# First edge layer of a graph network on one core: where VectorE builds the matrix of equal owners within a round

## The reference, cut to what matters

```python
Wh = h @ W + b
Wr, Wc = Wh[row], Wh[col]
sim = sum(Wr * Wc) / maximum(norm(Wr) * norm(Wc), EPS)
base = adj_v * sc * (row != col)
prop_pos = segment_sum((base * relu(sim))[:, None] * Wc, row)
prop_neg = segment_sum((base * -relu(-sim))[:, None] * Wc, row)
x = x + scale * (coeff[0] * prop_pos + coeff[1] * prop_neg + coeff[2] * Wh)
```

## Time and profile before

| what | value |
|---|---|
| median of three executions | 2410.95 us |
| the profiled execution, its own time | 2418.68 us |
| its span | 2416.6 us |
| busy, share of the span | PE 65%, DVE 64%, ACT 36%, POOL 70% |
| first edge layer, in the trace | about 206 to 1503 us of the span |
| POOL busy from 500 to 1500 us | 809.97 us of 1000 |
| DVE busy from 500 to 1500 us | 514.08 us of 1000 |
| granted TensorE clock from 500 to 1500 us | 0.50 |

### The profile page before, as it was taken

The page is one execution under the profiler, slowest core; times in us unless marked ns, Lnnn a source line. Parts: engine busy times, 40 slices in busy tenths (PEclk is TensorE's granted clock), DMA queues, the critical chain, the costliest instruction groups (busy, mean ns, idle before and its releaser), DMA issues. The chain is left out here.

```text
span 2416.6 us, 57279 instructions
## 1 busy us (share of the span) xinstructions
PE 1562.8 (65%) x16004; PEld 1340.6 (55%) x16004; DVE 1553.3 (64%) x5636; ACT 864.0 (36%) x3093; POOL 1695.9 (70%) x1413
## 2 busy tenths in 40 slices
PE   4886755455555555555555550005999999997998
PEld 2555645455554545545455550004999999994554
DVE  5995655555555454554545552794999999995554
ACT  3773322222222222222222221462333333334665
POOL 2775888888888888888888886746777777761322
PEclk9996555555555555555555555556999999999999
DMA  3775544444444444444444432565555454534664
GB/s 100 251 247 172 114 82 80 77 83 75 84 79 78 84 74 85 80 77 83 75 86 73 84 47 18 170 221 146 128 124 126 124 126 124 126 81 119 188 188 145
DMA packets 342563, 273.11 MB, mean 113 GB/s; under 512 B 144834, under 2 KB 273514, under 8 KB 342484
## 3 DMA queue, kind: packets, MB, share of 16 engines
q1 hardware_dynamic: 259028, 233.22, 33.2%
q0 software_dynamic: 81536, 38.61, 15.0%
q10 hardware_dynamic: 1920, 0.37, 0.1%
HBM read 206.69 MB, written 65.34 MB: 113 GB/s over the span
## 5 line engine op out<-in xcount | busy, mean ns | idle before, releaser
L1117 POOL DMA_INDIRECT x<-e_sums,e_to x392 | 623.4, 1590 | 126.4 <-issue 118.6
L1352 PE MATMUL bank<-e_parts,e_same 128*128 128x64 bf16 x2940 | 172.8, 240 | 586.7 <-DVE e_parts L1211 586.7
L1304 PE MATMUL bank<-e_window,e_onehot 128*128 128x64 f32 x2352 | 525.0, 422 | 16.8 <-DMA e_window<-wh 16.8
L1304 PEld LDWEIGHTS bank<-e_window,e_onehot 128*128 128x128 f32 x2352 | 511.7, 332 | 16.9 <-DVE e_onehot L1143 16.9
L1102 POOL DMA_INDIRECT e_ends<-wh,e_ids x392 | 425.2, 1085 | 132.8 <-issue 102.1
L1352 PEld LDWEIGHTS bank<-e_parts,e_same 128*128 128x128 bf16 x2940 | 159.4, 129 | 602.8 <-issue 602.8
L829 POOL DMA_INDIRECT e_near_source<-h,e_near_ids x392 | 394.8, 1007 | 129.8 <-issue 117.4
L1250 ACT ACTIVATE e_sq<-e_ends 128x64 f32<-128x64 f32 x784 | 188.6, 241 | 686.0 <-DMA e_ends<-wh,e_ids 685.9
L1175 DVE SCALAR_TENSOR_TENSOR e_prod<-e_ends 128x64 f32<-128x64 f32 x392 | 65.7, 223 | 370.8 <-DMA e_ends<-wh,e_ids 370.8
L939 PE MATMUL bank<-e_near_to_edge,e_near_window 128*64 128x128 f32 x2352 | 153.4, 281 | 171.2 <-DMA e_near_window<-h 171.2
L939 PEld LDWEIGHTS bank<-e_near_to_edge,e_near_window 128*64 128x64 f32 x2352 | 130.0, 139 | 177.6 <-DVE e_near_to_edge L850 171.6
(11 more groups left out here) (150 smaller groups left out, 2860.9 us busy)
## 6 DMA issues: line engine op xcount, KB each, us to landing
e_window<-wh SPq DMA_DIRECT2D x392, 96.0 KB
e_near_window<-h SPq DMA_DIRECT2D x392, 96.0 KB
e_owners<-ends SPq DMA_DIRECT2D x98, 256.0 KB, 2.9
n_x<-x SPq DMA_DIRECT2D x98, 256.0 KB, 3.0
n_x<-in_x_dram SPq DMA_DIRECT2D x49, 256.0 KB, 2.8
wh<-n_wh SPq DMA_DIRECT2D x49, 256.0 KB, 2.0
x<-n_x SPq DMA_DIRECT2D x49, 256.0 KB, 2.3
e_rel<-rel SPq DMA_DIRECT2D x98, 128.0 KB, 3.2
```

The costliest lines, as they stand in the source:

```text
L1117: pool.indirect_dma_start(out=added_tab, out_offset=bass.IndirectOffsetOnAxis(ap=t.to[s][:, j:j + 1], axis=0), in_=t.sums[s][:, j, :], in_ ...
L1304: last = nc.tensor.matmul(bank[s % 2][:, j * D:(j + 1) * D], onehot, window, start=w == 0, stop=w == WK - 1)
L1352: last = nc.tensor.matmul(bank[6 + s % 2][:, i * D:(i + 1) * D], t.same[s][:, same_block(j, i), :], t.parts[s][:, part, j, :], start=j == ...
```

## The change

In DVE's list for the first edge layer the part `compare` now comes before `match`, with every lag as it was. So in step i DVE first makes the dot products of group i-2 and then the matrix of equal owners of group i-1. It used to be the other way round.

```diff
-        parts = [(-3, leave), (0, ahead), (-3, low), (-1, match), (-2, compare), (-2, address), (-2, weigh)]
+        parts = [(-3, leave), (0, ahead), (-3, low), (-2, compare), (-1, match), (-2, address), (-2, weigh)]
```

## The result

The changed kernel takes 2393.63 us in the median of five runs (2391.51 to 2400.18), the kernel before 2411.21 us in the same comparison. The ratio is 0.9921, with a 95% interval from 0.9903 to 0.9938. By this ratio it is 19 us faster, between 15 and 23. (The medians alone differ by 17.6 us.) The forecast was 2392 us.

The account below looks back on a forecast made before the run. POOL's own instructions bound the first edge layer, lengthened 0.63 us a round by DVE running beside them. With 0.43 us instead, 0.20 us less over 94 rounds is 19 us: 2410.95 to 2392 us, range 2372 to 2427 us.

Parts of the forecast that it names:

- DVE's chain: DVE's work from `weigh` on comes 0.95 us later; T is the first dot product's start; DVE does not become the bound.
- The landing: Loads issued earlier no longer lie beside the last gather, so L falls to 2.4 to 3.0 us in most rounds.
- L: Time from the start of a round's last gather to the dot products; sets where DVE's work falls on POOL's.
- The third scatter: At L = 2.5 us POOL's third scatter starts at T+2.55 in the last `same`, losing 0.1 us.
- The rival in which scatters pay more than gathers save: Landing stays; third scatter starts in the 384-column `same`, second gather in the one-hot; 5 to 15 us slower; chance 0.28.
- The rival in which the whole matrix blocks a scatter: A scatter loses to all four `match` rows, 1.1 us a round; 80 us slower, 2491 us; chance 0.03.
- The sum: POOL's surplus from running beside DVE falls from 0.63 to 0.43 us a round, 19 us over 94 rounds; chance 0.43.
- theory 3: From the experiments: taking the matrix of equal owners off the gathers is the gain, whatever L is.
- theory 4: Formed after e8: the one-hot's place against the first gather is what changed; long gathers come from one-hot with `low` behind.
- `match` costs the gathers 0.25 us a round: Surplus before: 0.12 us on the third gather, 0.10 us on 27 long gathers, 0.03 us on the gather behind.
- the balance of 0.24 us on scatters against 0.25 us on gathers: With places spread evenly, `match` costs scatters now what it cost gathers; the no-change rival, 2411 us, chance 0.18.
- list for each L: Loss a round by L: 0.3 us at 2.5, 0.4 or 0.5 at 2.9, 0.9 at 3.5, about 0.2 above 4.2.

Follow-up runs that it names:

- e2: Changed kernel with SP's owners load and those behind it held until `low` of the slot's last group is done; ratio 1.0007, 13.08 us a round.
- e1: Kernel before, with SP's owners load and those behind it released early, once the slot's last addresses are written; ratio 1.0052, 13.21 us a round.
- e8: Kernel before with the matrix of equal owners cut to 8 columns per instruction, so sums are not the layer's; ratio 1.0017, 13.06 us a round.
- e9: Changed kernel with the matrix cut to 8 columns per instruction, so sums are not the layer's; 2411.27 us, ratio 0.9984, 13.10 us a round.
- e10: e1 with the left-over computed twice more, 0.7 us more DVE work ahead of the one-hot; 2385.92 us, ratio 0.9881, 12.78 us a round.
- e5: The changed kernel itself again, on another chip; ratio 0.9895, 12.89 us a round.
- e7: Changed kernel with the two address instructions ahead of the matrix instead of behind it; ratio 0.9962, 12.88 us a round.
- e6: Changed kernel reordered: dot products, matrix, row numbers and one-hot, weighing, then addresses; ratio 0.9860, 12.66 us a round.

## Why the prediction was right, and where it wasn't

**The bound and the mechanism: right.** POOL's own instructions and the constant gaps between them are the length of the layer, before and after (226.7 and 226.8 us of gaps), and the change acted through the instructions' lengths alone.

**DVE's chain: right.** `weigh` starts at T+3.03 (T+3.25 forecast), the one-hot at T+6.23 (T+6.15), and the norms are no wait any more. `weigh`'s second instruction, which takes 0.17 us alone, takes 0.45 us in the rounds shown, so the 0.2 us by which it started early were lost again behind it. The cover held: ACT, PE and SP lost nothing that POOL saw.

**The landing: right.** L fell from 3.55 to 2.49 us, and 92 of 93 rounds are under 3.3 us. `owners` is issued at T+2.9, as forecast.

**The third scatter: right, and cheap.** It starts at T+2.57 (T+2.55) in the last `same` and loses 0.04 us in the mean; I had 0.1 us. The rival in which scatters pay more than gathers save needed L over 3.2 us, and e2 shows a piece of it: at L up to 3.3 us and more the period is 13.08 us. The rival in which the whole matrix blocks a scatter is refuted by the rows at 577.23: 0.49 us lost of 1.8 us that remained.

**The sum: right to 0.06 us a round.** 0.43 us a round forecast, 0.37 us measured, between my 0.3 us for L = 2.5 and 0.4 us for L = 2.9. In the layer 23.7 us were gained where 19 us were forecast; that the ratio of the runs says 19 us as well is no better agreement, as its interval goes from 15 to 23 us. The first gather, in three rounds of four about 0.13 us behind the one-hot's start, loses 0.26 us in the mean (I had 0.2 us).

**Where the gain lies.** The table puts each gather's time over 0.94 us to the DVE instruction that is under way when the gather starts, in us a round. A long gather that starts in the one-hot and waits for `low` as well is counted under the one-hot. The last column is the same for the scatters, over their 6.32 us.

| kernel | one-hot | `same` | `leave`, `low`, `msgs` | others or none | on scatters |
|---|---|---|---|---|---|
| before | 0.28 | 0.12 | 0.16 | 0.03 | 0.04 |
| after | 0.26 | 0.00 | 0.05 | 0.03 | 0.04 |
| e1 | 0.56 | 0.12 | 0.00 | 0.01 | 0.00 |
| e8 | 0.42 | 0.01 | 0.04 | 0.03 | 0.04 |
| e9 | 0.54 | 0.00 | 0.00 | 0.04 | 0.00 |
| e10 | 0.20 | 0.03 | 0.00 | 0.03 | 0.00 |

Of the 0.26 us that the change gained, 0.12 us are the matrix off the gathers (theory 3), and 0.12 us are `leave`, `low` and `msgs`, which the gathers rarely meet now that the rounds hold one place. The one-hot's price fell by 0.02 us. The place of the one-hot (theory 4) has a price all the same: at the same L its place is worth 0.20 us with the matrix cut (e9 against after, 13.10 to 12.89) and 0.43 us with the matrix beside the gathers (e1 to e10). But theory 4 doesn't describe what changed here, because the kernel before was not locked in the bad place: only 26 of its 93 first gathers start 0.8 to 1.0 us into the one-hot, 18 start within its first 0.2 us, and 47 start ahead of it. In after, 88 start within its first 0.2 us. What the new place did is to avoid the bad one: with a short landing alone (e1) the one-hot costs 0.56 us.

**The step that failed: "`match` costs the gathers 0.25 us a round".** It is 0.12 us, by the table and by e1 against e9. I had put 0.10 us of it on the 27 long gathers, since the one in the earlier trace rows ended with the 512-column `same`. e2, e8 and e9 have the same gather with a short matrix or none behind `low`, and its mean is 1.58 us in e9 and 1.59 us in before: it comes from the one-hot and `low` without a gap. So the balance of 0.24 us on scatters against 0.25 us on gathers had a wrong term. The forecast did not rest on it: it had the places of the one-hot and the scatters in its list for each L, and came out right by that list.

**A reading that failed without harm.** From the earlier trace rows I took it that a gather which starts in the one-hot ends 0.12 us behind the whole one-hot. The one-hot is three instructions, and the gather ends 0.91 us behind the first of them (e10) or, when it starts in the second or third, 0.89 us behind that one (e1). For a start in the first instruction both give the same end, which is where the list for L = 2.5 us had it. For the starts at 0.9 us my reading gives no loss at all, where the rows have 0.3 to 0.7 us. That the list needed only the case in which both agree was luck.

**Left open.** In before, e1, e8 and e9 together 282 gathers start in the third instruction of the one-hot. 74 of them end 0.81 to 0.89 us behind that instruction, and 208 end 0.82 to 0.89 us behind `low`, which follows without a gap. Their starts overlap (0.90 us into the one-hot at 588.75 in e1, 1.27 us long, and 0.90 us at 535.48, 1.60 us long). Why some get in ahead of `low` and most don't, no run here shows.

## What to carry to other kernels

Where POOL's own instructions are the bound, DVE's program is a layout problem: ask of each DVE instruction which POOL instruction starts while it runs, and price that overlap from rows, one instruction at a time, as a merged row hides where the single ones end. Less DVE work can be slower (e9, 19 us over after in this layer) and more of it faster (e10, 40 us under e1), because rounds that follow each other's landing lock in one place, good or bad. And where two events end together in one row, look for a second row in which they don't, before one is called the cause of the other.

## What the runs showed of the hardware

- A POOL gather of 0.94 us takes 1.27 us when it starts 0.13 us into a one-hot of three instructions of 0.48 us, 1.14 us at 0.25 us, and 1.56 us at 0.93 us with `low` behind. It ends 0.89 to 0.91 us behind the DVE instruction in which it started, or behind `low` where it waits for two. A gather that starts within the first 0.07 us of the one-hot takes 1.01 us (after, e5, e7). A scatter of 1.56 us that starts inside a two-input DVE instruction loses about the rest of it less 0.1 us (0.49 us where 0.62 us were left) and nothing for those that follow. The Trainium skill, "SBUF — State Buffer", section "SBUF: two separate sides", has the port pair that the two engines share, held for a whole instruction. The rows agree with this for the DVE instruction under way. They do not for POOL's, as three more `same` run beside the scatter at 577.23, and that the long gather is two holds in a row no run here proves.
- It goes the other way too: a one-hot that takes 1.27 us beside gathers takes 1.59 us in the row of e6 below, where a scatter starts ahead of it, and a tensor_scalar of four columns takes 0.45 us in place of 0.17 us. The rows are of e6 and of after:

```profile
495.41 1.55 POOL L1117 DMA_INDIRECT x<-e_sums,e_to  x1 [0.30 <-issue]
495.60 1.59 DVE L1143 TENSOR_SCALAR e_onehot<-e_rel,in_window 128x512 f32<-128x512 f16 x3
```

```profile
520.03 1.56 POOL L1117 DMA_INDIRECT x<-e_sums,e_to  x1 [0.30 <-issue]
520.60 0.47 DVE L1186 TENSOR_SCALAR e_small<-e_small 128x4 f32<-128x4 f32 x1
```

  The tensor_scalar ends 1.04 us behind the scatter's start, at 521.07, and in the round before it, started at 507.74, 1.09 us behind it, as if it waited for something that the scatter does at that time. What that is, no run here shows.
- PE's granted clock was 0.50 in this layer in after as in before (240 to 1440 us), which is the lower of its two levels, 1.2 GHz, with PE 54% busy.
